# Experts' second matmul with h stationary, its last chunks run inside the next tile, the bias added by GpSimd

## The reference

```python
x = input_features.reshape(-1, Df)               # 4096 tokens of 256
aff = x @ centroids.T
assign = jnp.argmax(aff, axis=1)                 # one expert a token
order = jnp.argsort(assign); xs = x[order]; es = assign[order]
alpha = jax.nn.sigmoid(jnp.take_along_axis(aff[order], es[:, None], axis=1))
for e in range(nE):                              # 8 experts, w1 1024x256, w2 256x1024
    h = _layernorm(xs, ln_g[e], ln_b[e])
    h = jax.nn.relu(h @ w1[e].T + b1[e])
    ye = xs + h @ w2[e].T + b2[e]
    y = y + jnp.where((es == e)[:, None], ye, 0.0)
out_sorted = alpha * y + (1.0 - alpha) * xs      # = xs + alpha * (h @ w2.T + b2)
```

## Time and profile before

| | |
|---|---|
| median of 3 runs | 1029.28 us |
| profiled execution | 1030.96 us, of which span 1029.1 us |
| PE busy | 930.2 us (90%), granted clock 0.947 on average |
| DVE busy | 696.1 us (68%) |
| ACT busy | 745.3 us (72%) |
| POOL busy | 300.5 us (29%) |

### The profile page before, as it was taken

The page is one execution under the profiler, slowest core; times in us unless marked ns, Lnnn a source line. Parts: engine busy times, 40 slices in busy tenths (PEclk is TensorE's granted clock), DMA queues, the critical chain, the costliest instruction groups (busy, mean ns, idle before and its releaser), DMA issues. The chain is left out here.

```text
span 1029.1 us, 17730 instructions
## 1 busy us (share of the span) xinstructions
PE 930.2 (90%) x5301; PEld 513.2 (50%) x5301; DVE 696.1 (68%) x1836; ACT 745.3 (72%) x1414; POOL 300.5 (29%) x349
## 2 busy tenths in 40 slices
PE   5599999999999999999999998996179999999992
PEld 2134444444444433333333333332169998998991
DVE  5367777887778777265575664585447887787783
ACT  1488878787878869898899985893046766866861
POOL 4042314041322112002122222123333444443443
PEclk9699999999999989999999996997579999999996
DMA  8988689959696786696696684551262543453450
GB/s 218 208 224 225 154 223 262 230 175 210 195 230 171 198 219 119 155 261 108 149 186 134 132 159 86 125 119 42 70 227 105 179 178 115 158 205 124 164 216 31
DMA packets 74844, 172.04 MB, mean 167 GB/s; under 512 B 16657, under 2 KB 36039, under 8 KB 64712
## 3 DMA queue, kind: packets, MB, share of 16 engines
q1 hardware_dynamic: 67944, 156.36, 59.9%
q0 software_dynamic: 6496, 14.16, 4.0%
q10 hardware_dynamic: 320, 0.52, 0.2%
HBM read 122.23 MB, written 53.73 MB: 171 GB/s over the span
## 5 line engine op out<-in xcount | busy, mean ns | idle before, releaser
L773 ACT ACTIVATE probs<-sc 128x512 f32<-128x512 f32 x1024 | 530.3, 609 | 123.4 <-DVE sc L864 83.9
L508 PE MATMUL sc<-qst,kst 57*128 57x512 f32 (+1 forms) x1024 | 262.1, 474 | 14.6 <-DMA qst<-s_qk 12.7
L864 DVE TENSOR_TENSOR sc<-sc,strip 128x308 f32<-128x308 f32 (+1 forms) x512 | 192.0, 429 | 100.1 <-PE sc L508 98.8
L520 PE MATMUL ot<-probs,vals 128*32 128x512 f32 x1600 | 214.0, 607 | 0.1
L508 PEld LDWEIGHTS sc<-qst,kst 57*128 57x128 f32 (+1 forms) x1024 | 117.8, 188 | 177.9 <-ACT probs L773 132.6
L1735 ACT ACTIVATE f_h<-f_h_ps,par 128x384 f32<-128x384 f32 x104 | 60.8, 586 | 32.0 <-PE f_h_ps L1645 32.0
L1812 DVE TENSOR_TENSOR f_h_lo<-f_h,f_h_hi 128x384 fp32r<-128x384 f32 x104 | 66.5, 639 | 13.7 <-DVE f_h_hi L1810 5.7
L1893 POOL DMA_INDIRECT home<-s_x,get_ids x45 | 53.2, 1183 | 75.0 <-issue 42.6
L1810 DVE CAST f_h_hi<-f_h 128x384 fp32r<-128x384 f32 x104 | 37.0, 356 | 41.2 <-ACT f_h L1735 41.0
L520 PE MATMUL ms<-probs,vals 128*32 128x512 f32 x448 | 62.9, 637 | 0.0
L1906 POOL DMA_INDIRECT out<-f_normed,f_put_ids x39 | 43.0, 1103 | 64.6 <-ACT f_normed L1769 56.2
(11 more groups left out here) (189 smaller groups left out, 1619.5 us busy)
## 6 DMA issues: line engine op xcount, KB each, us to landing
s_qk<-w_hi SPq DMA_DIRECT2D x32, 512.0 KB, 7.1
strip<-in_w_all SPq DMA_DIRECT2D x16, 1024.0 KB, 7.9
f_raw<-in_w_all SPq DMA_DIRECT2D x14, 1024.0 KB, 6.7
s_x<-x SPq DMA_DIRECT2D x8, 1026.0 KB, 10.4
kst<-s_qk SPq DMA_DIRECT2D x32, 256.0 KB, 6.0
qst<-s_qk SPq DMA_DIRECT2D x32, 256.0 KB, 7.0
s_x_parts<-split SPq DMA_DIRECT2D x16, 512.0 KB, 3.1
kst<-s_ctx_parts SPq DMA_DIRECT2D x32, 256.0 KB, 6.1
```

Of the source, the lines that this page charges most:

```text
L508: nc.tensor.matmul(sc[j][:], kst[at:at + rows, i, P * c:P * c + P], qst[at:at + rows, i, :], start=True, stop=True).then_inc(scored, 1)
L520: last = nc.tensor.matmul(sums_bank(n, g)[32 * j:32 * j + 32, :], vals[:, c, 4 * g + j, :], probs[:, k % KEPT, j, :], start=(c == 0), stop ...
L773: nc.scalar.activation(probs[:, k % KEPT, j, :], sc[j][:], ACT.Exp, scale=scale).then_inc(exped, 1)
L864: nc.vector.tensor_tensor(sc[j][:, lo:hi], sc[j][:, lo:hi], band_backwards(rank_of(4 * g + j), at, hi - lo), ALU.add).then_inc(biased, 1)
```

## The change

1. `ffn2`: h is the stationary operand (128 tokens x 128 channels) and w2 the moving one (256 columns). A chunk is 9 matmuls of 256 columns instead of 6 of 384. y has tokens on partitions, in three banks. Only three banks are left for `ffn1`.
2. A tile's chunks 5, 6, 7 of `ffn2` run in the next tile, behind its `ffn1` of chunks 0, 1, 2.
3. `turn_out`, `keep_y`, `gate_rows`, `shift_rows` are gone. `turn_in` is in two halves, after chunks 3 and 5.
4. `relu` runs twice on ScalarE: once into the high part, once in full. VectorE's cast is gone.
5. `add_rows` on VectorE reads y from PSUM, multiplies by alpha and adds what GpSimd kept, one group at a time. `hat_out` goes from ScalarE to VectorE.
6. `keep_rows` on GpSimd: copy of alpha, b2 times alpha (three instructions), and twice the addition of the rows (two instructions with two inputs of 768 columns). It stands behind `inverse_deviation` now. b2 comes as 128 equal rows by a load of its own.
7. GpSimd's `finish` no longer begins with a drain.

```diff
             def ffn2(i, s, f):
...
                 pe.wait_ge(h_ready, FC * i + f + 1)
-                for d in range(DC):
-                    col = C * f + P * d
-                    for n, (w, x) in enumerate(((w_hi, h_hi), (w_hi, h_lo), (w_lo, h_hi))):
-                        last = nc.tensor.matmul(y_ps[d][:], w[s][:, 1, col:col + P], x[f % (LAG + 1)][:],
+                for t in range(TC):
+                    some = slice(P * t, P * t + P)
+                    if f == 0:
+                        wait(pe, have_res, TC * (i - 1) + t + 1)
+                    for n, (x, w) in enumerate(((h_hi, w_hi), (h_hi, w_lo), (h_lo, w_hi))):
+                        last = nc.tensor.matmul(y_ps[t][:], x[at][:, some], w[s][:, 1, col],
                                                 start=(f == 0 and n == 0), stop=(f == FC - 1 and n == 2))
...
             def step(i, s, n):          # TensorE
                 for f in range(FC):
                     ffn1(i, s, f)
                     if f >= LAG:
                         ffn2(i, s, f - LAG)
-                    if f == 1 and later(i):
-                        turn_out(i - 1)
-                    if f == 4:
-                        turn_in(i + 1, 1 - s, n + s)
-                for f in range(FC - LAG, FC):
-                    ffn2(i, s, f)
+                    elif later(i):
+                        ffn2(i - 1, 1 - s, FC - LAG + f)
+                    if f in (3, 5):
+                        turn_in(i + 1, 1 - s, n + s, f // 5)
...
             def relu(i, s, f):          # ScalarE
-                nc.scalar.activation(h[f % (LAG + 1)][:], h_ps[f % (LAG + 1)][:], ACT.Relu, bias=bias).then_inc(h_full, 1)
+                nc.scalar.activation(h_hi[at][:], h_ps[f % H_BANKS][:], ACT.Relu, bias=bias).then_inc(h_hi_ready, 1)
+                nc.scalar.activation(h[at][:], h_ps[f % H_BANKS][:], ACT.Relu, bias=bias).then_inc(h_full, 1)
...
                 for f in range(FC):     # ScalarE's step
                     relu(i, s, f)
                     if f in (0, 1):
                         split_w(i + 1, 1 - s, n + s, 0, f)
+                    if f in (3, 5):
+                        split_w(i + 1, 1 - s, n + s, 1, f // 5)
+                    if f in (4, 6):
+                        scale_in(i + 1, 1 - s, n + s, f // 6)
...
                 for f in range(FC):     # VectorE's step
+                    if f == 7:
+                        low_in(i + 1, 1 - s, 1)
+                    if f == 2 and later(i):
+                        for t in range(TC):
+                            add_rows(i - 1, 1 - s, t)
+                    low_h(i, f)
+                    if f in (0, 1):
+                        low_w(i + 1, 1 - s, 0, f, w1_lo_ready)
+                    if f == 3 and later(i):
+                        norm_out(i - 1)
+                    if f == 5:
+                        low_in(i + 1, 1 - s, 0)
+                    if f in (4, 6):
+                        low_w(i + 1, 1 - s, 1, f // 6, w2_lo_ready)
+                    if f == 5 and later(i):
+                        hat_out(i - 1)
...
             def keep_rows(i, s, n):     # GpSimd
-                nc.gpsimd.tensor_copy(keep[s][:], rows[s][:, :, 0:C + 1]).then_inc(kept, 1)
+                nc.gpsimd.tensor_copy(gate[s][:], rows[s][:, :, C]).then_inc(have_gate, 1)
+                wait(pool, have_gate, i + 1, pool_passed)
+                for t in range(TC):
+                    nc.gpsimd.tensor_scalar(keep[s][:, t, :], b2[s][:], gate[s][:, t:t + 1], None, ALU.mult).then_inc(gated_b2, 1)
+                wait(pool, gated_b2, TC * (i + 1), pool_passed)
+                nc.gpsimd.tensor_tensor(keep[s][:], keep[s][:], rows[s][:, :, 0:C], ALU.add).then_inc(added_once, 1)
+                wait(pool, added_once, i + 1, pool_passed)
+                nc.gpsimd.tensor_tensor(keep[s][:], keep[s][:], rows[s][:, :, 0:C], ALU.add).then_inc(kept, 1)
...
             def finish(i):              # GpSimd
-                pool.drain()
```

More of the change, by code:

```diff
@@ L33 @@
 LAG = 3
+H_BANKS = 3
 BEHIND, KEPT = 2, 4
@@ L37 @@
 W_COLS = DC * F
[L38 removed]
+PARAMS = 2 * DC + FC
 STEP = 16
@@ L1693, in step, with turn_in @@
+            def turn_in(i, s, n, d):
+                if d == 0:
+                    pe.wait_ge(gathered[s], 16 * TC * (n + 1))
+                wait(pe, xn_hi_ready, DC * i + d)
+                at = C + 1 + P * d
+                for t in range(TC):
+                    last = nc.tensor.transpose(turn_ps[d][:, P * t:P * t + P], rows[s][:, t, at:at + P], ident[:])
+                last.then_inc(in_mm, 1)
             def step(i, s, n):
@@ L1714, in split_w, with scale_in @@
                     act.wait_ge(ld_w[s], 32 * (n + s))
-                    wait(act, y_mm, FC * (i - 1))
+                    if m == 0:
+                        wait(act, h_mm, FC * (i - 1))
+                    else:
+                        wait(act, y_done, TC * (i - 1))
                 nc.scalar.activation(w_hi[s][:, m, some], raw[s][:, m, some], ACT.Copy).then_inc(w_hi_ready, 1)
-            def scale_in(i, s, n):
-                act.wait_ge(ld_par[s], 16 * (n + 1))
-                for d in range(DC):
-                    act.wait_ge(in_mm, DC * i + d + 1)
+            def scale_in(i, s, n, d):
+                if d == 0:
+                    act.wait_ge(ld_par[s], 16 * (n + 1))
@@ L1880, in finish @@
                     hat_last(i - 1, t)
-            low_in(0, 0)
+            for d in range(DC):
+                low_in(0, 0, d)
             tiles(dve, step, finish)
```

236 lines of the change are left out of this document (91 added, 145 removed).

## The result

The changed kernel takes 1052.5 us (median of 4, 1046.7 to 1056.5), the kernel before 1029.0 (median of 4, 1027.5 to 1029.9). The ratio is 1.0213, 95% interval 1.0168 to 1.0259: slower by 2.1%, and by 1.7 to 2.6% with the noise counted in. Forecast were 1046 us and a range of 1016 to 1060. The profiled execution has a span of 1051.1 us, against 1029.1.

What follows compares the result with a forecast made beforehand. TensorE was taken as the bound, with GpSimd's row work and VectorE's chain adding up at each tile's end. 776.3 + 11 x 21.3 + 35 = 1045.6 us of span, so 1046 us, range 1016 to 1060.

Steps and rivals of the forecast that it cites:

- the sum: Whole span: 776.3 to tile 1's start, 11 tiles of 21.3, 35 at the end, together 1045.6 us.
- What bounds it, and what is late next: Expert tiles: TensorE bounds, 9.7 us of waits before lone chunks go, then the next tile's start waits for low input.
- The chain without GpSimd: Tile's end: relus, low part, weights' subtraction, then low input let TensorE start the next tile after 18.4 us.
- GpSimd begins its row work 12.5 us into the tile: GpSimd in each tile: `keep_rows` stands behind the power, which waits for the previous tile's variance, so starts at 12.5.
- The cost of the products: GpSimd's `keep_rows`: three products of 256 columns at about 0.4 us each, bounds 0.28 and 0.83.
- The additions: GpSimd's `keep_rows`: two additions of 768 columns, 1.84 us each, within 5.1 us of row work.
- I treat the two as one resource: Tile's end: from 12.5 us, GpSimd's 5.1 and VectorE's 3.7 add up before the next start, 21.3 a tile.
- whichever issues second blocks: GpSimd against VectorE on SBUF: the later-issued instruction blocks fully; traces said to agree, with 1.16 and 0.40 us delay.
- the rival in which the last addition loses: Tile's end: VectorE runs chunk 6, weights and input while GpSimd's second addition waits; tile 19.45, all 1025, chance 13%.
- The clock: Expert tiles: TensorE's 3 us idle lowers the clock; tile 22.9, all 1063, or 1052 in a third; chance 17%.
- The tail: From tile 12's start to the span's end: some 35 us instead of 39.6, bounds 33.5 and 39.6.
- The gain of 4.6 for the drain: Kernel's end: without the drain the list decides when GpSimd's last power starts, shortening the end by 4.6 us.

Runs made afterwards that it cites:

- e2: The changed kernel without GpSimd's two additions of 768 columns a tile, leaving the gathered rows out of the result: 1020.6 us, ratio 0.9884 to the kernel before.
- e8: The changed kernel with the second half of the low input ahead of the weights' subtraction on VectorE: 1027.0 us, ratio 0.9968 to the kernel before.
- e11: The changed kernel with one of GpSimd's two additions dropped by halving alpha and normalising with EPS / 4: 1043.1 us, ratio 1.0124 to the kernel before.
- e6: The kernel before without the drain of GpSimd ahead of its last powers, nothing else changed: 1031.9 us, ratio 1.0015 to the kernel before.
- e9: The changed kernel with GpSimd's copy of alpha and products ahead of the power, the additions behind it: 1059.9 us, ratio 1.0288 to the kernel before.
- e4: The changed kernel with GpSimd's row work (copy of alpha, products, additions) behind the three scatters: 1064.7 us, ratio 1.0324 to the kernel before.
- e1: The changed kernel with the drain of GpSimd put back ahead of its last powers: 1054.0 us, ratio 1.0207 to the kernel before.

## Why the prediction came out as it did

The time, 1046 for 1052, is nearer than its steps. Against the profiled span, the sum was 776.3 + 234.3 + 35; measured 777.5 + 229.5 + 44.1.

- **What bounds it, and what is late next: right.** The waits of the earlier trace rows are gone (1.6 us are left, 2.8 of 12.5 were expected), and TensorE waits ahead of `ffn1(0)` for the low input. Matmuls of 256 columns run at a pitch of 0.12, and TensorE works 17.8 us of an undisturbed tile (19.97 less 2.12 of idle; 18.2 forecast). The chain without GpSimd was forecast at 18.4 a tile; with the additions out (e2) it is 18.54.
- **GpSimd begins its row work 12.5 us into the tile: right,** 12.7 (876.91 - 864.20).
- **The cost of the products: mis-sized.** 1.04 us each against 0.4 (bounds to 0.83). A product with a scalar per partition is not priced by a copy of the same columns (0.28 for a third of the copy in the earlier trace rows). The additions were right: 1.65 to 1.73 where nothing held them, against 1.84.
- **"I treat the two as one resource": this step failed.** It gave 21.3 a tile; undisturbed tiles take 19.96. With the measured start and durations (0.45 + 0.21 + 3.07 + 0.18 + 1.65 + 0.18 + 1.73 = 7.5 for GpSimd) it would give 12.7 + 7.5 + 3.7 = 23.9, further off still: the products' error of 1.9 us had hidden part of it. The products ran beside the low part of chunk 5 and the norm (0.76 and 1.49 us for these), and the second addition fell behind the input. In these tiles only one meeting is in the chain: weights (started first), addition, input. e8 and e11 show it: moving one subtraction is worth 1.0 us a tile at the full clock, 1.9 with what the clock gives back, and removing one addition is worth nothing there. Only in tiles 0 and 1, where the first addition started ahead of the weights, did both additions stand in front of the input, as the sum has it. Nor do the starts in the profile tell who is held, though I wrote that rows 7 and 8 agree with "whichever issues second blocks": in the earlier trace rows the subtraction had started 0.45 us first and was held, in tile 5 the weights had started 0.10 first and the addition was held. For most tiles what came is the rival in which the last addition loses, priced 19.45, with the first addition still in it.
- **The clock: the rival came as well**, in 5 of 11 tiles, 8.6 us; I had put it at 17% and had not put it into the sum. It fell after idles of 2.11 to 3.45 us, never in the eleven tiles of e8 with 0.64 to 1.19, and it costs 1.5 us each time but one (2.5), about as in the earlier trace rows.
- **The tail: the largest term that was missing.** 35 forecast, 44.1 measured. The gain of 4.6 for the drain does not exist (e6: -0.2). Of the 9.1 us, 6.2 are the drain's time at the end, and 2.9 the later last scatter, of which some 1.5 are one more fall of the clock, in tile 12 (0.52 above). The earlier trace rows showed 6.98 us of idle, and I took idle in front of an instruction for time that goes with it.

So one term was 11 x (21.3 - 19.96) = 14.7 too large, and 8.6 (clock), 1.3 (second addition in tile 1), 9.1 (tail) and 1.2 (start) were missing, 5.5 too little in sum. That the number is near is luck, and the sign owes much to it. With the undisturbed tile as measured and my own start and tail, the sum is 776.3 + 11 x 19.96 + 35 = 1030.9, only 1.8 us above the kernel before. The step that is sound, GpSimd holding the input, outweighs the gain of the other parts by 15.6 - 9.6 = 6.0 us, and my gain for the drain, which does not exist, would have taken 4.6 of them back. The rest of the 22 us is the clock (8.6), the tail (4.5 longer than before), the second addition in tile 1 (1.3) and the later start (1.5).

## What to carry to other kernels

Look at which instruction of VectorE is the one that TensorE waits for, and keep GpSimd's reads off that one and off those in front of it in the queue: a hold of 1.4 us on the weights was free (e8), one of 2.6 on the norm was not (e9). The same work cost 20.9 or 19.0 us a tile by the order of two subtractions. A GpSimd instruction whose work is moved takes its queue along, so ask first what waits for the instruction behind it (e4, e9). A drain is paid somewhere: look at what stands at the very end of the span before counting its removal as a gain. And before a difference of 1 to 2 us between two kernels is put down to an edit, compare the granted clock of the two stretches (e1).
